# The update gate's sum over its two state parts moved from VectorE to TensorE in steps 10 to 15

## The reference

```python
def step(H, xs):
    xz, xr, xh = xs
    Z = sigmoid(xz + H @ Whz.T + bhz)
    R = sigmoid(xr + H @ Whr.T + bhr)
    H_tilda = tanh(xh + R * H @ Whh.T + bhh)
    H_new = Z * H + (1.0 - Z) * H_tilda
    Y = H_new @ Whq.T + bhq
    return H_new, Y
```

## Time and profile before

| what | value |
|---|---|
| median of 3 runs | 1256.75 us (1255.55 to 1257.06) |
| the profiled execution | 1256.6 us |
| its span | 1254.1 us |
| TensorE matmul busy | 1209.1 us, 96% |
| VectorE busy | 897.3 us, 72% |
| ScalarE busy | 444.5 us, 35% |
| mean granted TensorE clock | 0.961 of full |

### The profile page before, as it was taken

The page is one execution under the profiler, slowest core; times in us unless marked ns, Lnnn a source line. Parts: engine busy times, 40 slices in busy tenths (PEclk is TensorE's granted clock), DMA queues, the critical chain, the costliest instruction groups (busy, mean ns, idle before and its releaser), DMA issues.

```text
span 1254.1 us, 53718 instructions
## 1 busy us (share of the span) xinstructions
PE 1209.1 (96%) x22316; PEld 1179.8 (94%) x22316; DVE 897.3 (72%) x5772; ACT 444.5 (35%) x2246; POOL 72.3 (6%) x55
## 2 busy tenths in 40 slices
PE   5899999999999999999999999999999999999875
PEld 5789999999999999999999999999999999999864
DVE  4347777777777777777777777777777777777655
ACT  1023333333333333333333333333333333333322
POOL 3310000000000000000000000000000000000000
PEclk8799999999999999999999999999999999999855
DMA  8501001111100011011001111001111110111000
GB/s 332 219 24 28 18 14 28 29 29 28 29 21 10 28 28 29 28 28 28 4 27 29 29 28 29 29 6 26 29 28 29 29 28 6 26 28 25 7 6 6
DMA packets 44228, 44.90 MB, mean 36 GB/s; under 512 B 7736, under 2 KB 40768, under 8 KB 42704
## 3 DMA queue, kind: packets, MB, share of 16 engines
q1 hardware_dynamic: 42416, 39.80, 11.1%
q10 hardware_dynamic: 1344, 1.08, 0.3%
q0 software_dynamic: 224, 0.59, 0.2%
HBM read 36.75 MB, written 4.72 MB: 33 GB/s over the span
## 4 chain that ended last, share of the span: by engine, by line
PE 94%; DMA 2%; DVE 2%; ACT 1%; issue 1%; SPq 0%; POOL 0%; DVEq 0%; POOLq 0%
PE bank L379 52%; PE gate_rh L379 32%; PE gate_z L379 11%; DMA gates<-gates_t 1%; DMA gates_t<-comb_rows 1%; DVE state L1014 0%; DMA sw<-in_sw 0%; ACT rg L722 0%; DVE rhp L998 0%; ACT hin L722 0%; POOL expn L346 0%; DVE osb L943 0%; SPq L253 0%; DVE ge L900 0%; DVE zin L1008 0%
## 5 line engine op out<-in xcount | busy, mean ns | idle before, releaser
L379 PE MATMUL gate_rh<-state,whp 128*128 128x8 f16 x6144 | 250.6, 167 | 13.8 <-DVE state L1014 13.8
L379 PEld LDWEIGHTS gate_rh<-state,whp 128*128 128x128 f16 x6144 | 234.9, 97 | 27.9 <-DVE state L1014 16.1
L722 ACT ACTIVATE rg<-gate_rh 128x16 f32<-128x16 f32 x512 | 94.2, 184 | 463.4 <-PE gate_rh L379 463.4
L379 PEld LDWEIGHTS gate_rh<-rhp,whp 128*128 128x128 f16 x6144 | 229.6, 96 | 15.5 <-DVE rhp L998 10.4
L379 PE MATMUL gate_rh<-rhp,whp 128*128 128x8 f16 x6144 | 236.7, 167 | 7.4 <-DVE rhp L998 7.4
L998 DVE SCALAR_TENSOR_TENSOR rhp<-rg,hist 128x16 f16<-128x16 f32 x512 | 89.7, 175 | 167.4 <-ACT rg L722 158.9
L379 PE MATMUL gate_z<-state,whp 128*128 128x16 f16 x4096 | 180.5, 177 | 0.0
L379 PE MATMUL bank<-ge,rw 128*128 128x128 f32 x1024 | 166.5, 293 | 4.7 <-DVE ge L900 4.7
L722 ACT ACTIVATE zg<-zsum 128x16 f32<-128x16 f32 x512 | 110.5, 216 | 167.2 <-DVE zsum L1003 167.2
L379 PE MATMUL bank<-xt,rw 128*128 128x128 f32 x1024 | 167.4, 293 | 0.7 <-DVE sa L881 0.7
L1008 DVE TENSOR_SCALAR zin<-zg,nsscale 128x16 f32<-128x16 f32 x512 | 120.4, 235 | 55.9 <-ACT zg L722 38.6
(11 more groups left out here) (152 smaller groups left out, 1585.6 us busy)
## 6 DMA issues: line engine op xcount, KB each, us to landing
gates<-gates_t SPq DMA_DIRECT2D x30, 512.0 KB, 5.3
aw<-in_aw SPq DMA_DIRECT2D x4, 2048.0 KB, 20.6
xt<-in_xT SPq DMA_DIRECT2D x32, 128.0 KB, 5.1
out<-osb SPq DMA_DIRECT2D x32, 128.0 KB, 4.0
rw<-in_rw SPq DMA_DIRECT2D x2, 1024.0 KB, 11.2
sw<-in_sw SPq DMA_DIRECT2D x3, 512.0 KB, 6.2
gates<-gates_t ACTq DMA_DIRECT2D x2, 512.0 KB, 10.3
wh<-in_wh SPq DMA_DIRECT2D x3, 256.0 KB, 7.9
```

What stands on the lines that cost most here:

```text
L379: return pe.matmul(o, w, x, start=start, stop=stop, skip_group_check=True)
L722: return act.activation(o, i, f, **kw)
```

## The change

In steps 10 to 15 of every block (`Z12 = 10`) TensorE issues twelve update-gate matmuls of 8 columns instead of eight of 16. All of them add into plane 0 of gate_z; the product of the weights' low part with the state's low part is no longer formed. Four of the twelve stand in front of the wait for the state's low part and of the reset gate's last four, eight behind them. ScalarE reads the sum from PSUM behind `z_done`, and VectorE's sum over the planes isn't issued in these steps. Steps 0 to 9 keep the old form.

```diff
@@ step, TensorE
                 recur(pr, R, 0, parts, 1)
                 recur(pr, R, 1, parts, 1)
+                if s >= Z12:
+                    pz = z_ps[par][:, 0, :, now]
+                    recur(pz, Z, 0, parts, 1)
+                    pe.wait_ge(st_low, n)
+                    recur(pr, R, 0, parts, 0, r_done)
+                    recur(pz, Z, 1, parts, 1)
+                    recur(pz, Z, 0, parts, 0, z_done)
+                    return
                 pe.wait_ge(st_low, n)
                 recur(pr, R, 0, parts, 0, r_done)
@@ ScalarE
-                    act.wait_ge(zsum_done, n)
-                    func(zg[:], zsum[:], ACT.Tanh, scale=tanh_scale[Z]).then_inc(zg_done, 1)
+                    if s >= Z12:
+                        act.wait_ge(z_done, n)
+                        func(zg[:], z_ps[par][:, 0, :, now], ACT.Tanh, scale=tanh_scale[Z]).then_inc(zg_done, 1)
+                    else:
+                        act.wait_ge(zsum_done, m[1] * Z12 + s + 1)
+                        func(zg[:], zsum[:], ACT.Tanh, scale=tanh_scale[Z]).then_inc(zg_done, 1)
@@ VectorE
-                    dve.wait_ge(z_done, n)
-                    dve.tensor_reduce(zsum[:], z_now.rearrange("p a k c -> p k c a"), AX_X, ALU.add).then_inc(zsum_done, 1)
+                    if s < Z12:
+                        dve.wait_ge(z_done, n)
+                        dve.tensor_reduce(zsum[:], z_now.rearrange("p a k c -> p k c a"), AX_X, ALU.add).then_inc(zsum_done, 1)
```

More of the change, by code:

```diff
@@ L28 @@
 W_TOP, S_TOP = 14, 12
+Z12 = 10
 GATE_OPS = 14
```

## The result

The changed kernel takes 1259.73 us (median of 22 runs, 1256.98 to 1261.93). The kernel before, run beside it, takes 1257.07 (22 runs, 1254.31 to 1259.14). The ratio is 1.002 with a 95% interval of 1.0014 to 1.0027: 2.66 us slower, where 2.5 was forecast.

A forecast was written before the change was run, and what follows sets the result against it. TensorE's sequence of matmuls was taken to bound blocks 0 to 29, the loop over the engines blocks 30 and 31. 0.4 + 3.0 - 0.7 - 0.2 = +2.5 us, giving 1259.3 us; range 1255.4 to 1262.2.

The forecast's parts named there:

- TensorE, step 10: Step 10 of blocks 0 to 29: four extra matmuls with no wait to cover cost 0.10 us each time, 3.0 us.
- TensorE, steps 11 to 15: These steps of blocks 0 to 29: four matmuls fill the wait, 0.60 us before and after; 0.4 us more together.
- Who gains from 0.025? Not steps 11 to 15: The scan starting 0.025 us sooner was held not to help these steps, which start in TensorE's own rhythm.
- Step 0: Step 0 keeps the old order and its wait, and gains 0.025 us from the sooner scan; 0.7 us less.
- Blocks 30 and 31: Last two blocks, without filler: the loop decides, 0.3 us less, step 10 of block 30 pays 0.1; together 0.2 less.
- VectorE's pauses: Supposed to come at a fixed count of VectorE's instructions, so the change moves them; 1.5 us either way.
- (a): Rival: the loop, not TensorE's issue, decides in steps 11 to 15 and 0; 1255.5 us, not slower; chance 0.12.
- My test against it: Between the last filler and the next reset group: the unchanged 0.75 us was taken to show TensorE's rhythm.
- (b): Rival: the four matmuls don't cover the wait, 0.10 us in 150 steps, 15 us more, 1274; chance 0.06.
- (c): Rival: weight loads follow one another at their 97 ns, 74 us more, 1334; chance 0.02.
- The cover: Steps 11 to 15: four update matmuls stand in the low part's wait, which lasted about as long as they do.

The follow-up runs named there:

- e1_z11: The changed kernel with step 10 back in its old form, new form in steps 11 to 15 only; 1256.65 us against 1256.69 beside it, ratio 0.9998.
- e7_eight: The changed kernel without the last four of its twelve update matmuls in steps 10 to 15; 1259.1 us, ratio 1.0019.
- e2_behind: The changed kernel with its first four update matmuls moved from in front of the low part's wait to behind the reset gate; 1266.9 us, ratio 1.0081.
- e3_plane0: The kernel before without VectorE's sum in steps 10 to 15, matmuls unchanged, ScalarE reading plane 0 of gate_z alone; 1250.07 us, ratio 0.9948.
- v2_stt: The kernel before with zin computed by a scalar_tensor_tensor with a full tensor instead of a tensor_scalar, in all steps; 1251.15 us, ratio 0.9956.
- e5_memset: The changed kernel with a small VectorE memset where the sum was, in steps 10 to 15; 1258.83 us against 1256.31 beside it, ratio 1.0025.
- v2_again: v2_stt once more, unchanged, against the kernel before; 1252.06 us, ratio 0.997.
- v4_pad5: v2_stt with five VectorE memsets of spare columns added in the set-up; 1249.54 us, ratio 0.9955 to the kernel before.
- e4_all: The changed kernel with the new form in all sixteen steps; 1286.6 us, ratio 1.0246.

## Why the prediction was right

The sum was right, 2.66 us against 2.5, and so was its main part: step 10 pays for four matmuls that cover nothing. The mechanism was right only in part. For steps 11 to 15 I had TensorE's own rhythm decide, and the loop over the engines does. That term came out 0.7 too low, steps 1 to 9 weren't in the sum, and that the total still fits is in part luck.

**TensorE, step 10: right in size, right for one reason of two.** 3.0 forecast, 30 x 0.103 = 3.1 measured; e1_z11 gives all of it back. "Nothing hides this" holds. But "ScalarE and VectorE keep their places relative to it" tells half. e7_eight gives TensorE its 0.10 back, and step 10 still takes 2.19, since the reset gate's last four are 0.10 later and the loop with them. e2_behind leaves the reset gate where it was and puts the four behind it, and step 10 takes 2.187. Each of the two suffices, and they don't add up.

**TensorE, steps 11 to 15: the term that was mis-sized.** 0.4 us forecast, 30 x 0.036 = 1.1 measured. I had TensorE's rhythm decide in these steps, with a wait of 0.10 in it. e3_plane0 and v2_stt show that the loop through hin and the scan decided in the kernel before: it gets 0.025 shorter, and these steps go from 2.18 to 2.16. So "Who gains from 0.025? Not steps 11 to 15" was wrong. The change gives the loop these 0.025 and takes them back, since the low part is now due after 0.07 of wait and the four matmuls take 0.10. What is left over is 2.193. Of the 0.007 per step, some 0.004 is seen between the H gate's first matmul and the filler (0.311, was 0.307). Its cause stays open.

**Step 0: right.** -0.7 forecast, -0.6 measured: 0.027 off the reset gate, 0.005 back in the H gate. The scan starts 0.03 behind ScalarE's hin, as worked out from VectorE's hin being the late one. One of the two places read for that, the end of step 15 of block 14, wasn't an ordinary step: it is 0.13 longer than its median, because VectorE paused in front of the transpose ahead of zin.

```profile
625.00 0.21 DVE L876 STREAM_TRANSPOSE comb_rows<-comb 128x32 f32<-128x32 f32 x1 [0.26 <-issue]
```

That the scan starts 0.10 behind VectorE's hin when this one comes last is right all the same.

**Steps 1 to 9: not in the sum.** I cost them at nothing, and together they grew by 0.017 a block, 0.5 us. That is 0.002 a step, and I have no cause for it. Before they take 20.85 together and after 20.87, but e1_z11, e2_behind, e3_plane0, e5_memset and e7_eight, with the same steps 1 to 9, have 20.84 to 20.85. So it may belong to this one profiled execution and not to the change.

**Blocks 30 and 31: mis-sized by 0.2.** -0.2 forecast, +0.03 measured. The steps there got about 0.01 shorter, not 0.03; step 10 of block 30 pays its 0.10. With one execution of each I can't divide it further: in the other kernels' profiles these two blocks take 73.7 to 76.1, with the granted clock falling at other places of the work.

**VectorE's pauses: the guess holds.** They move with the count of instructions (e5_memset). They cost 1.07 us in blocks 1 to 28 where they cost 1.87 before, -0.8, within the 1.5 allowed. 3.1 + 1.1 - 0.6 + 0.5 = 4.1 for the blocks, less 0.8 of pauses, is 3.3; the table's 3.03 leaves 0.3 that I haven't divided (the pauses of blocks 0 and 29 aren't in the 0.8). My 2.5 came near because what I had too low, in steps 1 to 9 and 11 to 15, was largely paid back by pauses that I had at nothing. That they moved so as to give back and not to cost was luck.

**The rivals.** (a) was half true: its premise (the loop decides in steps 11 to 15) is shown by e3_plane0, v2_stt and e7_eight together, its result didn't come, because the four matmuls stand inside that loop. My test against it, the unchanged 0.75 of the last filler, couldn't tell: a wait for the low part in front of the reset gate's last four lengthens the loop without touching that distance. (b) didn't happen: the four cover the wait, and the reset gate's last four start 0.10 behind them (616.96, 617.06). e2_behind prices the uncovered wait at 0.07 a step. (c) is out: 768 more loads cost 3 us.

**The cover.** I costed the four matmuls in the wait at nothing since TensorE stands still there. That was nearly right (0.10 put into what was by then 0.07), but e7_eight shows that covering it brings next to nothing either: with four matmuls fewer the same wait stands in front of the H gate's low part. The loop takes 2.19 in the changed kernel, and TensorE's own work 0.60 + 0.53 + 0.30 + 0.75 = 2.18 (24 gate matmuls, four filler, the H gate, six filler), so taking from one alone gives next to nothing.

## What to carry to other kernels

Where two limits are equally long, a wait inside the busy engine's sequence is not free room: work put into it must not stand in front of what the loop waits for, and it pays only if the loop gets shorter too. To find which limit decides, take something from each alone (here e3_plane0 and e7_eight) rather than argue from one distance that would be the same under both. A cheaper form of the late operation (v2_stt and v2_again: 4.8 and 4.1 us faster) did what moving the sum to the full engine did not.

## What the runs showed of the hardware

**VectorE's pauses go by a count of 128 instructions.** I numbered the VectorE instructions that the trace records, and compared each start with the median for the same pair of neighbours. The 64th and each 128th after it stand out: before, 13 of these 49 are over 0.06 us late, and of the about 50 at any other place at most 3; in v2_stt 11 and 3, in v4_pad5 8 and 3, in e5_memset 10 and 8, in the changed kernel 8 and 6. But not every 128th instruction starts late; it depends on which one it is. Before, all nine that are a scan (L1014 or L1016) are late, by 0.24 to 0.37, and the seven that are L1018 by 0.04 to 0.06, while none of the 28 that are L998, L999, L1003, L1005, L1008 or L1010 is late by more than 0.004. One of these is number 192; it starts 0.084 behind L999, where the median is 0.086:

```profile
89.89 0.18 DVE L1003 TENSOR_REDUCE zsum<-gate_z 128x16 f32<-128x32 f32 x1
```

Why it shows at the scans and not there is open. A late start lengthens a step by 0.14 us at the fp32 scan, 0.23 to 0.27 in v2_stt's steps at the scan that makes the state's high part, 0.04 at the low part where the wait for it was open. A full block has 200 recorded instructions before, and 16 x 200 = 25 x 128, so the long steps repeat 16 blocks later (3 of blocks 2 and 18, 8 of 3 and 19, 9 of 8 and 24). The changed kernel has 194 a block and no such pattern. What the chip does in the pause, no run here shows.

**A small difference of form.** The zin with a constant per partition takes 0.235 us and the next instruction starts 0.145 behind its start; with a full tensor it takes 0.176 and the next starts 0.09 behind. So VectorE's hin starts 0.055 sooner. The scan gains only the 0.025 until ScalarE's hin is the later of its two inputs. The groups of instructions of v2_stt:

```profile
L1009 DVE SCALAR_TENSOR_TENSOR zin<-zg,nsfull 128x16 f32<-128x16 f32 x512 | 90.0, 176 | 55.2 <-ACT zg L723 38.2
```

**ScalarE reads PSUM sooner than SBUF.** The tanh of the update gate takes 184 ns from PSUM and 216 ns from SBUF; the groups of instructions of the changed kernel have both:

```profile
L731 ACT ACTIVATE zg<-zsum 128x16 f32<-128x16 f32 x320 | 69.1, 216 | 105.0 <-DVE zsum L1017 105.0
...
L731 ACT ACTIVATE zg<-gate_z 128x16 f32<-128x16 f32 x192 | 35.3, 184 | 0.0
```

**An fp16 matmul with its load costs 0.025 us for 8 columns as for 16**, into either bank. In e4_all twelve of 8 columns in place of eight of 16 cost 0.096 more in each of steps 1 to 9, 0.024 for each of the four. The Trainium skill ("TensorE: Matmul & The Clock Gate", section Back-to-back issue gap) gives about 25 ns as a floor for 1 to 64 columns; the trace agrees, with 12 in 0.30.
